# Four stages of a twelve-stage decoder reordered: a load order, one product's place, two biases' places, and the start of an attention loop

## The reference

```python
# L0_attn (mLSTM, 8 heads, D = 128)
q, k, v, o_preact = x @ Wq.T, x @ Wk.T, x @ Wv.T, x @ Wog.T
i_pre, f_pre = soft_cap(x @ Wi.T + bi), soft_cap(x @ Wf.T + bf)
...                                   # gated recurrence over time gives h
y = (sigmoid(o_preact) * (layernorm(h) * ln_w + ln_b)) @ Wout.T
# L2_xattn (one head, context of 1601 rows in each of 16 batches)
q, k, v = query @ Wq + bq, key @ Wk + bk, value @ Wv + bv
out = softmax(q @ k.T / sqrt(E)) @ v
# L2_attn (its attention is not used; a projection and an MLP are left)
x = x + gamma1 * (ln(x) @ proj_w.T + proj_b)
out = x + gamma2 * (ln(gelu(ln(x) @ fc1_w.T + fc1_b)) @ fc2_w.T + fc2_b)
# L3_attn (16 heads of 8; half of each head of q and k is rotated by cos, sin)
out = softmax(causal(rope(q) @ rope(k).T / sqrt(8))) @ v @ Wc
```

## Time and profile before

| what | value |
|---|---|
| median of three runs | 2926.3 us |
| profiled execution | 2925.77 us, span of its records 2924.0 us |
| mean granted PE clock in it | 0.929 of full speed |
| busy PE / DVE / ACT / POOL | 2574.9 / 1790.1 / 1633.0 / 1406.2 us |
| L0_attn | 510.82 to about 585 us |
| L2_xattn | 1632.09 to about 1759 us |
| L2_attn | 1759.69 to about 1826 us |
| L3_attn | 2745.09 to about 2855 us |

### The profile page before, as it was taken

One profiled execution on the slowest core, in us unless ns is written; L12 is line 12 of the kernel. 1 busy time (PEld: TensorE's weight loads), 2 busy tenths in 40 slices (PEclk: granted clock), 3 DMA queues, 4 the chain that ended last, 5 costly groups with the idle time before them and its releaser, 6 DMA issues. The chain is left out here.

```text
span 2924.0 us, 43865 instructions
## 1 busy us (share of the span) xinstructions
PE 2574.9 (88%) x16307; PEld 2148.7 (73%) x16307; DVE 1790.1 (61%) x3689; ACT 1633.0 (56%) x2848; POOL 1406.2 (48%) x1114
## 2 busy tenths in 40 slices
PE   5999997687999999999959694868999999999767
PEld 4899997476999999999847563765666666667546
DVE  7888874445555555555535446346887888878352
ACT  4888883335666666666613242325666666666332
POOL 1887783112666666666600250205565665655040
PEclk9999998788999999999969897887999999999885
DMA  3323320013111111110010330220000000000000
GB/s 108 104 83 90 104 81 13 14 30 86 35 35 35 35 35 35 35 35 24 12 49 1 94 90 16 59 59 18 24 24 13 24 13 24 24 13 1 25 1 15
DMA packets 222574, 117.83 MB, mean 40 GB/s; under 512 B 21368, under 2 KB 217632, under 8 KB 222368
## 3 DMA queue, kind: packets, MB, share of 16 engines
q1 hardware_dynamic: 222368, 115.11, 14.2%
HBM read 100.39 MB, written 13.64 MB: 39 GB/s over the span
## 5 line engine op out<-in xcount | busy, mean ns | idle before, releaser
L812 POOL TENSOR_TENSOR L_xattn_held<-L_xattn_held,L_xattn_shift 128x512 f32<-128x512 f32 (+1 forms) x613 | 763.8, 1287 | 290.2 <-ACT L_xattn_shift L732 290.0
L532 PEld LDWEIGHTS L_xattn_acc<-L_xattn_rows,L_xattn_held 128*128 128x128 f32 (+2 forms) x5120 | 618.1, 192 | 34.4 <-DVE L_xattn_mixed L915 8.8
L532 PE MATMUL L_xattn_acc<-L_xattn_rows,L_xattn_held 128*128 128x129 f32 (+2 forms) x5120 | 627.5, 275 | 5.2 <-DVE L_xattn_mixed L915 5.2
L936 DVE TENSOR_TENSOR L_xattn_running<-L_xattn_ring,L_xattn_running 128x512 f32<-128x512 f32 (+1 forms) x384 | 264.1, 688 | 270.1 <-PE L_xattn_ring L514 258.6
L1532 POOL TENSOR_TENSOR L_xattn_projected<-L_xattn_along,L_xattn_crossed 128x512 f32<-128x512 f32 (+1 forms) x256 | 272.2, 1074 | 289.7 <-DVE L_xattn_crossed L1588 287.7
L722 ACT ACTIVATE L_xattn_held<-L_xattn_held 128x512 f32<-128x512 f32 (+2 forms) x640 | 401.2, 632 | 0.2
L715 ACT COPY L_xattn_held<-L_xattn_ring 128x512 f32<-128x512 f32 (+1 forms) x416 | 243.9, 586 | 226.7 <-DVE L_xattn_running L936 192.6
L512 PE MATMUL L_xattn_ring<-L_xattn_queries_hi,L_xattn_keys_hi 128*128 128x512 f32 (+2 forms) x640 | 280.6, 439 | 3.4 <-DVE L_xattn_keys_lo L840 2.0
L514 PE MATMUL L_xattn_ring<-L_xattn_queries_hi,L_xattn_keys_lo 128*128 128x512 f32 (+2 forms) x640 | 253.6, 396 | 0.0
L513 PE MATMUL L_xattn_ring<-L_xattn_queries_lo,L_xattn_keys_hi 128*128 128x512 f32 (+2 forms) x640 | 252.8, 395 | 0.0
L1274 PE MATMUL L_xattn_sums<-L_xattn_probT,L_xattn_rows 128*128 128x256 f32 (+2 forms) x896 | 247.3, 383 | 0.6 <-ACT L_xattn_mixed L1438 0.6
(11 more groups left out here) (564 smaller groups left out, 4864.6 us busy)
## 6 DMA issues: line engine op xcount, KB each, us to landing
L_xattn_raw<-in_ctx SPq DMA_DIRECT2D x16, 768.0 KB
context_normalised<-L_xattn_fresh SPq DMA_DIRECT2D x16, 768.0 KB
L_xattn_rows<-context_normalised SPq DMA_DIRECT2D x16, 768.0 KB
L_xattn_fresh<-in_ctx SPq DMA_DIRECT2D x16, 768.0 KB
L_xattn_rows<-in_ctx SPq DMA_DIRECT2D x16, 768.0 KB
L_xattn_staged<-in_ctx SPq DMA_DIRECT2D x16, 768.0 KB
L_xattn_xhat<-context_normalised SPq DMA_DIRECT2D x16, 768.0 KB
L_ffn_w<-in_L_ffn_W SPq DMA_DIRECT2D x2, 896.0 KB, 5.5
```

The lines of the kernel that those rows point to most:

```text
L532: mm = nc.tensor.matmul(acc[:, c // 2, c % 2 * WIDE:(c % 2 + 1) * WIDE], held[0:n, u % 2, k, c * P:(c + 1) * P], rows[0:n, b % 2, k, :], s ...
L812: nc.gpsimd.tensor_tensor(tile, tile, shift[0:keys_of_tile[k]], ALU.subtract).then_inc(shifted, 1)
L936: seen = nc.vector.tensor_tensor(most, bank, most, ALU.max)
```

## The change

In L2_xattn the four weight loads are issued before pair 0's context, bv gets a semaphore of its own, and its add moves from the start to the end of DVE's stream. In L0_attn, Wog and Wout get their own semaphore; their transposes move ahead of the gates' transposes, ACT's two copies of them ahead of the copies of v, and the product for the output gate ahead of the scans' transposes; the sigmoid moves behind `keep_sums(7)`. In L2_attn the biases are multiplied by gamma and added to the residual ahead of the products, so that one DVE operation is left out after each. In L3_attn the two `y_twice` copies stand between the copies of q and k, the rotation is done on four tiles at a time, k is transposed before q and both go into the score banks, and DVE spreads the first two batches of k itself while POOL starts with the third.

```diff
 # L2_xattn, SP
-            load_staged(0, 0)
             for dst, src in ((wq, "Wq"), (wk, "Wk"), (wv, "Wv")):
                 sp.dma_start(dst[:], w[src]).then_inc(w_loaded, 16)
...
-            sp.dma_start(bv_rows[:], w["bv"].partition_broadcast(P)).then_inc(w_loaded, 16)
+            load_staged(0, 0)
+            sp.dma_start(bv_rows[:], w["bv"].partition_broadcast(P)).then_inc(bias_loaded, 16)
             load_staged(1, 1)
 # L0_attn, PE
+            pe.wait_ge(out_w_loaded, 16 * 2)
+            for n, rows in enumerate((wog_rows, wout_rows)):
+                turn = nc.tensor.transpose(bank[3][:, n * D:(n + 1) * D], rows[:], core.ident[:])
+            turn.then_inc(out_w_turned, 1)
             pe.wait_ge(gates_ready, 1)
...
+            pe.wait_ge(out_w_kept, 1)
+            for t in range(TILES):
+                mm = nc.tensor.matmul(bank[2 + t // 4][:, (t % 4) * D:(t % 4 + 1) * D], yT[:, t * P:(t + 1) * P], wogT[:],
+                                      start=True, stop=True)
+            mm.then_inc(og_done, 1)
             pe.wait_ge(scanned, 1)
 # L0_attn, ACT
             keep_sums(PAIRS - 2)
+            keep_sums(PAIRS - 1)
             act.wait_ge(og_done, 1)
...
-            keep_sums(PAIRS - 1)
 # L2_attn, DVE (the end of the stage in the same manner, with fc2_b and gamma2 on lat)
+            for name_b, gamma in (("proj_b", "gamma1"), ("fc2_b", "gamma2")):
+                nc.vector.tensor_tensor(row[name_b][:], row[name_b][:], row[gamma][:], ALU.mult)
+            dve.drain()
+            nc.vector.tensor_tensor(x[:], x[:], over_tiles(row["proj_b"][:], TILES), ALU.add)
             dve.wait_ge(proj_done, 1)
             for half in range(2):
                 nc.vector.tensor_tensor(z[:, 4 * half:4 * half + 4, :], bank[2 + half][:].rearrange("p (t d) -> p t d", d=D),
-                                        over_tiles(row["proj_b"][:], 4), ALU.add)
-            dve.drain()
-            nc.vector.tensor_tensor(z[:], z[:], over_tiles(row["gamma1"][:], TILES), ALU.mult)
+                                        over_tiles(row["gamma1"][:], 4), ALU.mult)
 # L3_attn, PE
-            pe.wait_ge(rot_ready, TILES)
-            pe.wait_ge(v_kept, 4)
+            pe.wait_ge(rot_ready, 2)
...
-                    turn = nc.tensor.transpose(bank[j][:, i * P:(i + 1) * P],
-                                               qk_rot[:, t, j // 2].rearrange("p h d -> p (h d)"), core.ident[:])
+                    turn = nc.tensor.transpose(score[j // 2][:, (j % 2) * BANK + i * P:(j % 2) * BANK + (i + 1) * P],
+                                               qk_rot[:, t, 1 - j // 2].rearrange("p h d -> p (h d)"), core.ident[:])
...
-                pe.wait_ge(k_spread, 2 * t + 2)
+                if t == 0:
+                    pe.wait_ge(k_first, 1)
+                else:
+                    pe.wait_ge(k_spread, 2 * t)
 # L3_attn, ACT
-            for copy in range(2):
-                last = nc.scalar.copy(y_twice[:, :, copy, :], yT[:].rearrange("p (b j) -> p b j", j=SEQ))
...
+                if t in (2, 5):
+                    act.wait_ge(yT_kept, 2)
+                    nc.scalar.copy(y_twice[:, :, t // 3, :], yT[:].rearrange("p (b j) -> p b j", j=SEQ)).then_inc(twice_ready, 1)
 # L3_attn, POOL (wait for rotT_kept 2 where it was 4)
-            for b in range(BATCHES):
+            for b in range(2, BATCHES):
 # L3_attn, DVE, between the second and the third of four v_diag groups
+                if j == 2:
+                    dve.wait_ge(rotT_kept, 2)
+                    for b in range(2):
+                        spread = nc.vector.tensor_tensor(k_diag[:, b], over_tiles(kT[:, b * SEQ:(b + 1) * SEQ], NH),
+                                                         over_last(own_head[:], SEQ), ALU.mult)
+                    spread.then_inc(k_first, 1)
```

More of the change, by code:

```diff
@@ L1740, in _ @@
             during(PAIRS - 3, 1)
-        LOADS = 5
+        LOADS = 4
         @block.tensor
@@ L1960, in _ @@
             normalize_dve(nc, dve, y[:], lat[:], square[:], stats, var_ready, std_ready, 1).then_inc(y_ready, 1)
-            dve.wait_ge(w_loaded, 16 * LOADS)
-            nc.vector.tensor_tensor(lat[:], lat[:], over_tiles(bv_rows[:], TILES), ALU.add)
             def take():
@@ L2015, in _ @@
             step(PAIRS - 1, 1, last=True)
+            dve.wait_ge(bias_loaded, 16)
+            nc.vector.tensor_tensor(lat[:], lat[:], over_tiles(bv_rows[:], TILES), ALU.add)
+            dve.drain()
             dve.wait_ge(out_done, 1)
@@ L2541, in _ @@
             turn.then_inc(gates_turned, 1)
-            pe.wait_ge(late_loaded, 16 * 4)
-            for n, rows in enumerate((wog_rows, wout_rows)):
-                turn = nc.tensor.transpose(bank[3][:, n * D:(n + 1) * D], rows[:], core.ident[:])
-            turn.then_inc(out_w_turned, 1)
+            pe.wait_ge(out_w_kept, 1)
[3 more added lines that the diff above has]
+            mm.then_inc(og_done, 1)
             pe.wait_ge(scanned, 1)
@@ L2551, in _ @@
             turn.then_inc(back_turned, 1)
-            pe.wait_ge(out_w_kept, 1)
-            for t in range(TILES):
-                mm = nc.tensor.matmul(bank[2 + t // 4][:, (t % 4) * D:(t % 4 + 1) * D], yT[:, t * P:(t + 1) * P], wogT[:],
-                                      start=True, stop=True)
-            mm.then_inc(og_done, 1)
             def shifts(p):
@@ L2627, in _ @@
             kept.then_inc(k_kept, 1)
+            act.wait_ge(out_w_turned, 1)
+            nc.scalar.copy(wogT[:], bank[3][:, 0:D])
+            nc.scalar.copy(woutT[:], bank[3][:, D:2 * D]).then_inc(out_w_kept, 1)
             act.wait_ge(v_done, 1)
@@ L2635, in _ @@
             kept.then_inc(v_kept, 1)
-            act.wait_ge(out_w_turned, 1)
-            nc.scalar.copy(wogT[:], bank[3][:, 0:D])
-            nc.scalar.copy(woutT[:], bank[3][:, D:2 * D]).then_inc(out_w_kept, 1)
             act.wait_ge(back_turned, 1)
@@ L3089, in _ @@
                 kept.then_inc(hidT_dve, 1)
+            nc.vector.tensor_tensor(lat[:], lat[:], over_tiles(row["fc2_b"][:], TILES), ALU.add)
             dve.wait_ge(out_done, 1)
@@ L3092, in _ @@
                 nc.vector.tensor_tensor(z[:, 4 * half:4 * half + 4, :], bank[2 + half][:].rearrange("p (t d) -> p t d", d=D),
-                                        over_tiles(row["fc2_b"][:], 4), ALU.add)
-            dve.drain()
-            nc.vector.tensor_tensor(z[:], z[:], over_tiles(row["gamma2"][:], TILES), ALU.mult)
+                                        over_tiles(row["gamma2"][:], 4), ALU.mult)
             dve.drain()
@@ L3124, in latent_attention_stage @@
         qk_rot = s.sb("qk_rot", [P, TILES, 2, NH, DH])
-        turned = s.sb("turned", [P, 2, NH, DHE])
+        turned = s.sb("turned", [P, 4, 2, NH, DHE])
         qT, kT = s.sb("qT", [P, TOKENS]), s.sb("kT", [P, TOKENS])
@@ L3327, in _ @@
             dve.wait_ge(loaded, 16 * LOADS)
-            for t in range(TILES):
-                dve.wait_ge(qk_kept, t + 1)
-                cols = qk[:, t].rearrange("p n h c -> p (n h) c")
-                out = qk_rot[:, t].rearrange("p n h c -> p (n h) c")
-                side = turned[:].rearrange("p n h c -> p (n h) c")
+            for half in range(2):
+                tiles = slice(4 * half, 4 * half + 4)
+                dve.wait_ge(qk_kept, 4 * half + 4)
+                cols = qk[:, tiles].rearrange("p t n h c -> p (t n h) c")
+                out = qk_rot[:, tiles].rearrange("p t n h c -> p (t n h) c")
+                side = turned[:].rearrange("p t n h c -> p (t n h) c")
                 nc.vector.tensor_copy(out[:, :, 0:DHE], cols[:, :, 0:DHE])
-                nc.vector.tensor_tensor(out[:, :, DHE:DH], cols[:, :, DHE:2 * DHE], over_tiles(angle[:, 0, :], 2 * NH), ALU.mult)
-                nc.vector.tensor_tensor(side, cols[:, :, 2 * DHE:UP], over_tiles(angle[:, 1, :], 2 * NH), ALU.mult)
+                nc.vector.tensor_tensor(out[:, :, DHE:DH], cols[:, :, DHE:2 * DHE], over_tiles(angle[:, 0, :], 4 * 2 * NH), ALU.mult)
+                nc.vector.tensor_tensor(side, cols[:, :, 2 * DHE:UP], over_tiles(angle[:, 1, :], 4 * 2 * NH), ALU.mult)
                 dve.drain()
```

20 lines of the change are left out of this document (10 added, 10 removed).

## The result

The changed kernel takes 2909.9 us (median of ten runs in two sets, 2906.2 to 2917.3) where the kernel before takes 2927.5 (median of 53 runs, 2920.1 to 2931.9). Taken beside runs of the kernel before, the ratio was 0.9944 (interval 0.993 to 0.9958) in the first set and 0.9946 (0.9932 to 0.9959) in the second: 16 us faster, between 12 and 20. Forecast were 2913.0 and a gain of 13.3. The mean granted clock barely moved, 0.932 for 0.929.

The account below looks back on a forecast made before the run. Late inputs and operation order inside four barrier-ended stages were taken as the bound. Terms 2.0 + 1.9 + 2.7 + 2.6 + 4.1 = 13.3 us off 2925.77 gave 2912.5, stated as 2913.0; 65% for 2909 to 2917, range 2906 to 2920.

Parts of the forecast that it names:

- three cases of the clock: L0_attn, head: clock rises at the same moment, gain 1.0; forecast gain 2.0; product keeps it high, gain 3.1.
- a term for the clock only as a loss: L2_attn, within the clock rival: PE's low clock after pauses takes 0.6 us of the stage's 2.6 gain.
- (a): L3_attn: y_twice copies no longer ahead of the first copy of q and k; at most 1.5 us, taken as 1.0.
- (b): L3_attn: rotation on four tiles at a time, v 3.0 us behind the last copy in place of 3.46; 0.5 us.
- (c): L3_attn: transposes wait only for PE's own products, not v_diag's second half; start 2782.7 in place of 2785.20.
- (d): L3_attn: the second copy, now of k, ends 2.57 us behind the start of the transposes, at 2785.3; 1.7 us earlier.
- (e): L3_attn: DVE's two k_diag operations run beside POOL's and take 4.0 us, between 2.4 and 4.7.
- The rival there: L3_attn, k_diag: POOL first each time, k ready after 6.2 us, stage gain 1.9; 7% as the DVE and POOL rival.
- The clock takes a part back: All four stages: PE stays at 1.2 GHz for a while after pauses; gain 8.5 us, kernel 2918; 15%.
- DVE and POOL hold each other up: L3_attn: k_diag operations go one behind the other, 6.2 us in place of 4.0; sum 11.1, kernel 2915; 7%.
- slow loop of L2_xattn: L2_xattn: context lands with PE cold, loop clock stays low, 10.6 us more per pair; slower than before, 2934; 2%.
- edits without effect: L0_attn's head and L2_xattn gain 0.2 us together in place of 4.7, product or w late; 2918; 3%.

Follow-up runs that it names:

- the kernel where kT came earlier: The changed kernel with PE's transposes of rotated q and k ahead of the second half of its v products in L3_attn; 2909.7 us.
- two variants with a shorter L3_attn (105.5 and 106.0): Changed kernel with PE's transposes ahead of the second half of v (105.5), 2909.7 us; with POOL behind DVE's k_diag pair (106.0), 2909.3 us; both together, 2903.5 us.

## Why the prediction was right, point by point

The sum is nearer than its parts. By the medians of the profiles the four stages give 3.4, 3.6, 4.2 and 2.0 us, 13.2 in all, where 3.9, 2.7, 2.6 and 4.1 were forecast, 13.3: two terms too small and one too large cancel, and that is luck.

**L0_attn, head.** Forecast 2.0 us, measured 2.3 at the loop's start (27.21 to 24.94). The order of events was as written, `shiftT` late next. The 0.25 us for the two weight transposes was not lost: the gates' transposes came 0.2 later, but `shiftT` was ready 24.84 us after the start in both profiles. Of the three cases of the clock, it was the one in between: the product kept the clock high for itself and PE then lost it during the first pair; 1.6 us were left at the last sums. In three of the four profiles in which the scans came 0.4 us later or more, the stage took 73 us, 1.4 more.

**L0_attn, tail.** Forecast 1.9, measured 2.0 (2.96 to 0.96).

**L2_xattn.** The time of the context was forecast as 10.9 us after the first DMA and measured as 10.37. The delay by four issues was right (the context's first issue came 1.80 us after the stage's), and the transfer with its tail was 0.5 us shorter than reckoned. The clock took more than the 0.2 of the forecast ahead of the scores: they started 2.9 us earlier where the context was turned 3.5 earlier, since turning it took longer (26 transposes in 5.86 us, before it 25 in 4.69). It gave 0.6 back in the loop's first round (13.88 us between the first two groups of scores, before it 14.51). The stage is 3.6 us shorter against 2.7, above the forecast and inside its bounds of 1.5 and 4.8.

**L2_attn.** The mechanism is right and the size is not: 2.6 by the two operations was counted correctly, but the stage with its edits is 4.2 us shorter by the medians of the profiles. 0.4 of the difference is the shorter idle of DVE, and 0.9 the clock, which rose 3.2 to 3.9 us after the start of fc1's product in the ten profiles with the edits and 4.8 to 5.3 in the four without; with them PE's pause ahead of the transposes of the second layernorm is shorter (7.9 us in all ten, 9.3 to 9.7 in the four). That the shorter pause brings the earlier rise is argued from this pair of facts; no run changed the pause alone. The forecast had a term for the clock only as a loss (0.6). The 5.9 us of the single pair of profiles held 1.7 of a slow draw besides.

**L3_attn.** That the medians of the timed runs beside the others lie 4.1 us apart, the forecast itself, is luck: the ratios give 1.8, the profiles' medians 2.0 for the stage. Up to the scores' start, where 4.1 were forecast, the pair of profiles shows 2.2, and 1.0 of that is lost behind it (63.40 us from there to the stage's end, before it 62.37). Link by link up to the scores, forecast and measured, in us earlier: (a) y_twice, 1.0 and -1.0; (b) rotation, 0.5 and 0.6; (c) transposes not behind `v_diag`, 1.0 and 0.8; (d) k kept, 1.7 and 2.0; (e) k spread, 0.0 and -0.3. **Step (a) failed.** The prediction read "PE's first product was already there" from the start of PE's row; the row is a group of products at the lower clock. After, ACT's first copy starts 1.68 us behind the group's start (2758.96 - 2757.28), when its first product is done; before, that would have been 25.6 us after the stage's start, and y_twice held it until 25.8. All but 0.2 us of the copies had been hidden. The other seven copies of q and k each waited for PE, so there was no more to win. Among them, y_twice costs: at the clock that both profiles had (0.79 and 0.80) the copies ended 8.62 us after PE's start where it had been 8.00. So 0.6 of the -1.0 is the edit's own; the rest is PE's product, which started 24.29 us after the stage's start and before 23.94, in a row of starts from 22.6 to 24.5 that follows no edit. The prediction's floor of 2775.6 for the last copy is not what its terms give either: 2769.05 and 5.84 us of copies are 2774.9. (e) was nearly right: DVE's pair took 4.07 for 4.0. The rival there, 6.2 us with POOL first, is real as well: 5.74 in the kernel where kT came earlier. So which engine comes first decides 1.7 us, and it hung on less than 0.1 us. On this the Trainium skill (SBUF — State Buffer, section "Who interferes with whom") says that the two engines take turns by whole instructions. The cases measured agree in kind: turns of 1.22 and 1.90 would make DVE's pair 4.3 us with DVE first and 6.2 with POOL first, and 4.07 and 5.74 were measured.

**The rivals.** *The clock takes a part back* did not come true as a whole: L2_attn gained where it saw a loss, and L2_xattn lost 0.5 ahead of its scores and won 0.6 behind. L0_attn's loop gave 0.7 back, and L3_attn's 1.0. That transposes raise the clock, as the earlier trace rows had it, holds: in this stretch of the changed kernel PE did nothing but transposes of L3_attn's weights. The row of the timeline, and one of the windows:

```profile
2739.65 4.98 PE L3181 MATMUL L_attn_bank<-all_ident,L_attn_down 128*128 128x128 f32 x24 [8.90 <-DMA L_attn_down<-in_L_attn_Wv_down]
```

```profile
2743.00:2745.00 2.00, 1.55 (x10) 0.86 (x9) 0.00 (x0) 1.68 (x4) 0.00 (x0) 0.98 0.23 53
```

The Trainium skill (TensorE: Matmul & The Clock Gate, section "Part 4: PE-mode transpose") rules that out; the measurement decides. *DVE and POOL hold each other up* came true in part: DVE came first, and the price was the 4.0 of the forecast, not the rival's 6.2. Neither the slow loop of L2_xattn nor the edits without effect appeared in any profile with them.

**What stays open.** Timed, the whole gives 16 to 18 us; the medians of the four stages and of L3_ffn give 14.3. The difference is within what single profiles scatter: the untouched stretch ahead of L0_attn took 510.3 to 514.6 us and L1_xattn 820.2 to 826.4 in the fourteen profiles. Why two variants with a shorter L3_attn (105.5 and 106.0) show no gain when timed alone, and 6 us together, is not settled either; four timed runs each are too few for it.

## What to carry to other kernels

Work an engine does in a row of grouped products ends piece by piece: before a copy is moved out of the way of the next one, look at the end of the first product at the clock it ran at, not at the row's start. Then look at where the copy goes, at both clocks: what lies in pauses while TensorE runs at 1.2 GHz can hold up the next copy when it runs at 2.4. Compare two profiles of such a stretch only where their granted clocks agree. Where GpSimd and the vector engine share an operation of two on-chip inputs, let the one on the critical path go first by a wait. Close a pause in front of TensorE and the product behind it may gain too; count that as a term with two signs, and read it from several profiles, since one pair of them can be 2 us off in a stage.

## What was unexpected of the hardware

Moving a product halved its time: sixteen matmuls took 2.05 us in ten of ten profiles where they followed PE's other work closely, 3.5 to 3.8 in four of four where PE had paused (L0_attn). The reverse was seen too: the changed kernel's L3_ffn kept PE busy through these windows at 1.2 GHz throughout.

```profile
2880.00:2885.00 5.00, 5.00 (x25) 5.00 (x25) 1.35 (x6) 1.85 (x6) 0.00 (x0) 0.50 0.02 3
...
2890.00:2895.00 5.00, 5.00 (x25) 5.00 (x25) 1.35 (x6) 1.76 (x7) 0.00 (x0) 0.50 0.00 0
```

And a copy of 512 elements on DVE takes 0.43 us where an operation with two inputs takes 0.68, so step (b)'s estimate of 0.7 for each was high for one of four.
